# Tail of a graph-attention and mixture-of-experts kernel: the last down projection in other banks by halves, its hidden rows turned inside expert 6's projection, two gathered blocks scaled by ScalarE

## What is computed

```python
xf = _layernorm(x.reshape(-1, Dd), ln_g, ln_b)
scores, idx = jax.lax.top_k(xf @ router_w, K)          # K = 2
gate = jax.nn.softmax(scores, axis=-1)
...
def _expert(x, g, b, W1, b1, W2, b2, Wo, bo):
    x = _layernorm(x, g, b)
    x1 = x @ W1 + b1
    x2 = jnp.clip(x @ W2 + b2, -20.0, 20.0)
    hidden = jnp.clip(x1 * (x2 * jax.nn.sigmoid(x2)), -10000.0, 10000.0)
    return jnp.clip(hidden @ Wo + bo, -10000.0, 10000.0)
...
out = sum over experts of gates_e[:, e, None] * _expert(xf, ...)
x = x + out
```

## Time and profile before

| | us |
|---|---|
| median of 3 executions | 535.42 |
| lowest, highest | 532.96, 538.06 |
| profiled execution, its own time | 531.92 |
| its span, first to last instruction | 530.0 |
| TensorE busy in the span | 502.4 |
| VectorE busy | 397.4 |
| ScalarE busy | 285.5 |
| GpSimd busy | 187.2 |

### The profile page before, as it was taken

One profiled execution on the slowest core, in us unless ns is written; L12 is line 12 of the kernel. 1 busy time (PEld: TensorE's weight loads), 2 busy tenths in 40 slices (PEclk: granted clock), 3 DMA queues, 4 the chain that ended last, 5 costly groups with the idle time before them and its releaser, 6 DMA issues.

```text
span 530.0 us, 6969 instructions
## 1 busy us (share of the span) xinstructions
PE 502.4 (95%) x2647; PEld 445.7 (84%) x2647; DVE 397.4 (75%) x652; ACT 285.5 (54%) x408; POOL 187.2 (35%) x168
## 2 busy tenths in 40 slices
PE   8999999999999999999999999769999999999985
PEld 8999999999999978788888887647887877877774
DVE  4848989953535335589887876886898898998996
ACT  4724134241342416498886216436788688697641
POOL 5000535665566003279885822150020000000363
PEclk9999999999999999999999999759999999999989
DMA  8489754444243442202006452475969989889463
GB/s 306 145 322 344 217 195 156 156 159 160 84 155 126 158 160 72 88 1 81 0 1 239 165 208 91 150 240 221 351 231 403 349 353 406 335 321 398 145 215 121
DMA packets 21075, 106.34 MB, mean 201 GB/s; under 512 B 4865, under 2 KB 5249, under 8 KB 11313
## 3 DMA queue, kind: packets, MB, share of 16 engines
q1 hardware_dynamic: 15472, 91.53, 46.1%
q0 software_dynamic: 3696, 7.96, 4.6%
q10 hardware_dynamic: 1872, 6.39, 3.6%
HBM read 98.97 MB, written 6.91 MB: 200 GB/s over the span
## 4 chain that ended last, share of the span: by engine, by line
PE 60%; DVE 21%; ACT 11%; DMA 3%; issue 3%; POOL 1%; SPq 0%; ACTq 0%; POOLq 0%; DVEq 0%
PE ps L1165 51%; DVE lo L757 12%; ACT hi L575 4%; ACT xg L674 3%; PE ps L1232 3%; PE ps L1171 2%; DMA raw<-in_wg 2%; PE ps L1260 2%; DVE eqt L844 1%; ACT xg_hi L678 1%; DMA xg<-z_rows,slot_tok 1%; DVE x2sg L1078 1%; DMA z_rows<-xfb 1%; PE ps L1297 1%; ACT x2sg L683 1%
## 5 line engine op out<-in xcount | busy, mean ns | idle before, releaser
L757 DVE TENSOR_TENSOR lo<-raw,hi 128x2048 fp32r<-128x2048 f32 x70 | 161.3, 2326 | 42.6 <-ACT hi L575 42.3
L575 ACT ACTIVATE hi<-raw 128x2048 fp32r<-128x2048 f32 x70 | 131.6, 1913 | 59.4 <-PE ps L1165 49.1
L460 POOL DMA_INDIRECT mask_rows<-colf,bits x48 | 61.9, 1290 | 92.3 <-DVE bits L852 44.1
L487 POOL TENSOR_SCALAR pr<-pr,small 128x384 f32<-128x384 f32 x48 | 59.0, 1247 | 54.6 <-DVE small L866 54.6
L1165 PE MATMUL ps<-xt_hi,lo 128*128 128x384 f32 x176 | 59.1, 336 | 0.0
L1165 PE MATMUL ps<-xt_hi,hi 128*128 128x384 f32 x176 | 59.1, 336 | 0.0
L1165 PE MATMUL ps<-xt_lo,hi 128*128 128x384 f32 x176 | 59.1, 336 | 0.0
L1165 PE MATMUL ps<-hi,xg_hi 128*128 128x512 f32 x128 | 52.0, 406 | 5.7 <-DVE lo L757 3.9
L1165 PE MATMUL ps<-lo,xg_hi 128*128 128x512 f32 x128 | 51.3, 401 | 0.0
L1165 PE MATMUL ps<-hi,xg_lo 128*128 128x512 f32 x128 | 51.3, 401 | 0.0
L1165 PE MATMUL ps<-t_hi,hi 128*128 128x384 f32 x128 | 43.1, 337 | 0.9 <-DVE t_lo L803 0.9
(11 more groups left out here) (221 smaller groups left out, 1078.2 us busy)
## 6 DMA issues: line engine op xcount, KB each, us to landing
raw<-in_wf SPq DMA_DIRECT2D x42, 1024.0 KB, 6.9
raw<-in_wg SPq DMA_DIRECT2D x28, 1024.0 KB, 4.9
xfb<-in_wf SPq DMA_DIRECT2D x6, 1024.0 KB, 7.4
src_i<-in_srcb ACTq DMA_DIRECT2D x4, 768.0 KB, 3.9
dst_i<-in_dstb ACTq DMA_DIRECT2D x4, 768.0 KB, 7.6
y_rows<-y SPq DMA_DIRECT2D x6, 512.0 KB, 3.0
xin<-in_x SPq DMA_DIRECT2D x3, 512.0 KB, 4.3
xres<-in_x SPq DMA_DIRECT2D x3, 512.0 KB, 4.2
```

The lines of the kernel that those rows point to most:

```text
L460: pool.indirect_dma_start(out=mbuf[:, :], out_offset=bass.IndirectOffsetOnAxis(ap=bits[:, 1, g:g + 1], axis=0), in_=colf[:, 5, g:g + 1], i ...
L487: pool.tensor_scalar(pr[:, h % 3, i, :], pr[:, h % 3, i, :], rinv[:, h % 3, i:i + 1], None, ALU.mult).then_inc(normalised, 1)
L575: act.activation(hi[SLOT[c]][:, :], raws[RAW[c]], ACT.Copy).then_inc(hi_done, 1)
L757: dve.tensor_tensor(lo[SLOT[c]][:, :], raws[RAW[c]], f32(hi[SLOT[c]][:, :]), ALU.subtract).then_inc(lo_done, 1)
```

## The change

Six things are changed, all in the tail. `down(7)` writes to B[1] and B[0] in place of B[3] and B[4], and no longer waits for `y_ready`; the sums of tile 0 go to B[3] and B[4] in place of B[0] and B[1]. `turn_hidden(7)` moves from behind `down(6)` to between its two halves. VectorE's `split_lo(75)` moves from in front of `hidden_lo(7)`, `store_y(6)` and the gate copy to behind them. Expert 7's clip is done by halves, each as soon as its half of the projection is done, with `y_rest` of the first half between them. Gathered blocks 0 and 1, rather than 4 and 5, are scaled by ScalarE and added by GpSimd; VectorE adds 2 to 5, and their places in its list change. ScalarE does its two scalings before, rather than after, the copies of `last_slots` and `y_hi` of expert 6. GpSimd's two additions stay behind all six gathers.

```diff
-        SUM_BANKS = [(0, 1), (5, 6), (2, 7)]
+        SUM_BANKS = [(3, 4), (5, 6), (2, 7)]
+        LAST_Y = [B[1], B[0]]
...
-                    for n in (4, 5):
+                    for n in (0, 1):
                         t, j = GATHERS[n]
-                        pool.wait_ge(rows_scaled, n - 3)
+                        pool.wait_ge(rows_scaled, n + 1)
                         ins = pool.tensor_tensor(xres[:, t, :], xres[:, t, :], yg[:, YG_SLOT[n], :], ALU.add)
...
             turned_hi(NE - 1, (NE - 1) % 2)
 
+            act.wait_ge(most_ready, 1)
+            for n in (0, 1):
+                t, j = GATHERS[n]
+                act.wait_ge(y_rows_in[j][t], 16)
+                act.activation(yg[:, YG_SLOT[n], :], yg[:, YG_SLOT[n], :], ACT.Copy, scale=r3[:, 8 + j, t:t + 1]).then_inc(rows_scaled, 1)
             act.wait_ge(last_oh_turned, 1)
...
-            act.wait_ge(most_ready, 1)
-            for n in (4, 5):
-                t, j = GATHERS[n]
-                act.wait_ge(y_rows_in[j][t], 16)
-                act.activation(yg[:, YG_SLOT[n], :], yg[:, YG_SLOT[n], :], ACT.Copy, scale=r3[:, 8 + j, t:t + 1]).then_inc(rows_scaled, 1)
...
                 dve.tensor_scalar(hh[:, :], hh[:, :], 10000.0, -10000.0, ALU.min, ALU.max).then_inc(h_ready, 1)
+                if e == NE - 1:
+                    split_lo(CHUNKS - 2)
+                    hidden_lo(NE - 1, (NE - 1) % 2)
+                    store_y(NE - 2, (NE - 2) % 2)
+                    dve.wait_ge(last_oh_turned, 1)
+                    dve.tensor_copy(slot_gate, B[7][:, 0:2]).then_inc(slot_gates, 1)
+                    split_lo(CHUNKS - 1)
+                    break
...
+            def last_y(half):
+                dve.wait_ge(chunk_used, CHUNKS - 1 + half)
+                dve.tensor_scalar(y[:, 1, halves[half]], LAST_Y[half], 10000.0, -10000.0, ALU.min, ALU.max).then_inc(y_half, 1)
+
+            def last_add(half, t):
+                dve.wait_ge(last_summed, NT * half + t + 1)
+                if t == 0:
+                    dve.wait_ge(tile_added, 1)
+                dve.tensor_tensor(xres[:, t, halves[half]], xres[:, t, halves[half]], B[SUM_BANKS[t][half]],
+                                  ALU.add).then_inc(out_ready, 1)
+
+            last_y(0)
             dve.wait_ge(y_hi_done, 1)
             y_rest(0, slice(0, D))
...
+            dve.wait_ge(y_hi_done, 2)
+            y_rest(1, halves[0])
+            last_y(1)
+            add_rows(2)
+            dve.wait_ge(y_hi_done, 3)
+            y_rest(1, halves[1])
+            for n in range(3, 6):
+                add_rows(n)
             for half in range(2):
                 for t in range(NT):
...
+                    last_add(half, t)
...
             def down(e, par, c):
+                to = LAST_Y if e == NE - 1 else B[3:5]
                 pe.wait_ge(ht_lo_done, e + 1)
-                if e:
+                if e and e < NE - 1:
                     pe.wait_ge(y_ready, e)
...
                     ins.then_inc(chunk_used, 1)
+                    if e == NE - 2 and part == 0:
+                        turn_hidden(NE - 1)
...
-                turn_hidden(e)
...
+                if e < NE - 1:
+                    turn_hidden(e)
+            turn_slots()
             down(NE - 1, 1, CHUNKS - 2)
```

More of the change, by code:

```diff
@@ L544, in _ @@
                         gather_rows(n)
-                    for n in (4, 5):
+                    for n in (0, 1):
                         t, j = GATHERS[n]
-                        pool.wait_ge(rows_scaled, n - 3)
+                        pool.wait_ge(rows_scaled, n + 1)
                         ins = pool.tensor_tensor(xres[:, t, :], xres[:, t, :], yg[:, YG_SLOT[n], :], ALU.add)
-                        if n == 4:
+                        if n == 0:
                             link(ins)
@@ L1104, in y_rest @@
                                          op0=ALU.mult, op1=ALU.subtract).then_inc(y_lo_done, 1)
[L1106 to L1111, removed]
+            halves = [slice(0, CW), slice(CW, D)]
+            def last_y(half):
[8 more added lines that the diff above has]
+            last_y(0)
             dve.wait_ge(y_hi_done, 1)
             y_rest(0, slice(0, D))
[L1114 to L1121, removed]
+            dve.wait_ge(y_hi_done, 2)
[6 more added lines that the diff above has]
+                add_rows(n)
             for half in range(2):
                 for t in range(NT):
[L1124 to L1128, removed]
+                    last_add(half, t)
             dve.wait_ge(out_ready, 2 * NT)
@@ L1361, in down @@
                     cols = slice(D + part * CW, D + (part + 1) * CW)
-                    pe.matmul(B[3 + part], selx[:, e % 3, :], brow[:, cols], start=True, stop=False)
+                    pe.matmul(to[part], selx[:, e % 3, :], brow[:, cols], start=True, stop=False)
                 for part in range(2):
@@ L1365, in down @@
                     for k in range(HT):
-                        ins = three(B[3 + part], (ht_hi[:, par, k, :], ht_lo[:, par, k, :]), weight(c + part, k), False, k == HT - 1)
+                        ins = three(to[part], (ht_hi[:, par, k, :], ht_lo[:, par, k, :]), weight(c + part, k), False, k == HT - 1)
                     ins.then_inc(chunk_used, 1)
+                    if e == NE - 2 and part == 0:
+                        turn_hidden(NE - 1)
             def turn_hidden(e):
@@ L1375, in turn_hidden, with turn_slots @@
                 ins.then_inc(h_turned, 1)
+            def turn_slots():
+                pe.wait_ge(last_oh, 1)
+                pe.wait_ge(xg_scaled, 2 * NE)
+                for j in range(2):
+                    for t in range(NT):
+                        pe.transpose(B[5 + j][:, t * P:(t + 1) * P], last_rows[:, j, t, :], ident[:, :])
+                for j in range(2):
+                    for t in range(NT):
+                        ins = pe.matmul(B[7][:, j:j + 1], last_rows[:, j, t, :], gates[:, t, LAST[j]:LAST[j] + 1], start=t == 0, stop=t == NT - 1)
+                ins.then_inc(last_oh_turned, 1)
             turn_tokens(0, 0)
```

## The result

Over 18 executions of each kernel the median goes from 533.41 to 536.63 us; the ratio is 1.0058, 95% interval 1.0037 to 1.0079, which is 3.1 us (2.0 to 4.2) of 533.41. The profiled execution takes 536.84 us (span 535.1) against 531.92.

What follows compares the result with a forecast made beforehand. VectorE, not TensorE, was taken as the bound: with no turn lost to GpSimd -0.6 us, with the turns worked out +2.7 us. Added to the 535.42 us median this gave 538.1 us, range 533.3 to 541.5.

Steps and rivals of the forecast that it cites:

- the rival without a collision: In the tail, GpSimd's additions and VectorE do not exclude each other: -0.6 us, 534.8 us, chance 0.13.
- the rival of a low clock: TensorE is granted 1.2 GHz from the new pause at 503.57 to the end: +5.5 us, 540.9 us, chance 0.07.
- Hidden, as said: ScalarE's earlier scalings and later copies add no time, unless block 1 lands later than 508.7.
- The sixth gather: On GpSimd, it starts at 510.26, 0.26 us after split_lo(75), and ends 0.8 us behind it, at 513.05.
- The rival with the gather in front: GpSimd's sixth gather precedes split_lo(75) and ends at 511.2; GpSimd's first addition ends at 514.5: +1.7 us, 537.1 us, chance 0.14.
- The collision: GpSimd's two additions take turns with VectorE's y_rest instructions, which wait for them: +2.7 us, 538.1 us, chance 0.66.
- VectorE's standing still in front of the first clip: VectorE waits for down(6) and the gate products, 1.3 us in all, with no add_rows to fill it.
- TensorE's sums: TensorE's sums before the final additions are done by 523 in any of the cases.
- The end: VectorE's six final additions end at 529.5, against 526.8 before.

Runs made afterwards that it cites:

- the run without the late add_rows: The changed kernel without GpSimd's two additions and without VectorE's add_rows of blocks 3, 4 and 5: tail 19.07 us, 528.71 us in one run.
- the run with TensorE's part alone: The kernel before with the change's new `down`, `turn_hidden`, `turn_slots` and their banks, other lists as before: tail 22.16 us, ratio to before 0.9979.
- the run with five blocks on VectorE: The changed kernel with VectorE adding five gathered blocks in another order and GpSimd only block 5, late: tail 21.15 us, ratio to before 0.9974.

## Why the prediction was right

The time, 536.63 us, lies in the range, and the change was forecast at +2.7 us: the tail shows +2.70. The range is wide enough for the rival without a collision too (534.8), so it is the steps below that tell the mechanism. The absolute 538.1 was 1.5 us too high, because the median of three executions that I added to, 535.42, lies 2.0 above that of 18, 533.41; the ratio of the times gives +3.1.

Step by step, with 2.34 us taken off the times after:

- TensorE: the transposes begin at 504.53 (504.62 expected), down(7) at 509.70 (509.86), its first half is clipped from 513.26 (513.2), its last product ends at 516.02 (516.0). The clock stayed at 1.00 in it, so the rival of a low clock did not occur.
- ScalarE: the second scaling ends at 508.79 (508.9 to 509.3), y_hi of expert 6 at 511.79 (511.9). Hidden, as said.
- The sixth gather starts at 510.28, 0.33 us behind split_lo(75), and takes 2.77 us in place of 0.94, ending 0.82 us behind the split. The rival with the gather in front did not occur in any of the five traces in which the two stand this way. The inference of the Trainium skill that the prediction weighed (SBUF — State Buffer, Who interferes with whom), that a tensor_tensor leaves descriptor making alone, does not hold for these gathers: 2.77 against 0.94 us. Whether the making of descriptors is held or the reading of the row numbers, which lie in SBUF, no run tells.
- The collision: turns at 515.48, 516.58, 518.84 and 519.39 (515.5, 516.6, 518.85, 519.4). Without it the tail is 22.23, 0.54 shorter than before (0.6 expected).
- VectorE's standing still in front of the first clip: 0.71, 0.67 and 1.02 us, 2.40 in all. The prediction's 1.3 us leave out the third wait; its sum goes by the times, which have it.
- TensorE's sums end at 523.69, later than the 523 that the prediction gave for every case, but 2 us ahead of the final additions.
- The end: 529.51 (529.5).

So two things make the result. VectorE comes last: the run without the late add_rows shows that its list bounds the tail, and the run with TensorE's part alone that the projection, which ends 2.6 us earlier (11.98 us behind the hh instruction with the change, 14.55 before), shortens the tail by only 0.61 us. And the two engines hold each other up: without GpSimd's additions the tail of the changed kernel is 3.24 us shorter.

This does not mean that the collision alone is the loss, since before had a hold too. What follows is an estimate from the timelines. Call idle the time in their brackets, and held what an instruction takes over the same shape unheld. VectorE is idle for 2.04 us of the tail before and for 2.40 after; it is held for 1.39 and for 3.58. What is left, its own work, is 19.3 and 19.5 us, and between 19.3 and 19.6 in every other run in which it has the same work. So longer holds make 2.2 of the 2.70 us. With TensorE's part alone, in the old order, VectorE is idle for only 0.20 us and held for about 2.7: against that the changed lists add 2.2 us of idle time and 0.9 us of holds. So the new order, which puts no add_rows in front of the first clip, has a price of its own. The run with five blocks on VectorE fits this: it fills that stretch, avoids the holds, and has the shortest tail of all the runs that do the whole work.

Not tried: the kernel before, or TensorE's part alone, without GpSimd's additions, which would show how the loss divides between order and collision; and VectorE's new order with GpSimd's additions neither left out nor moved but made by another engine.

## What to carry to other kernels

Before speeding up the engine that stands last on a chain, count what the next engine has still to do behind that point: work that was hidden under the slow step moves onto the path, instruction by instruction. Where VectorE and GpSimd both work on SBUF, lay their lists side by side and put GpSimd's two-input work beside VectorE's PSUM work or waits; an instruction whose duration varies twofold at the same shape, ending a fixed time behind one of the other engine, is the sign that they hold each other. Where such work is moved to the very end, check that the engine's closing does not then end the program later. When only the tail is changed, measure from a common mark in the trace, as what comes in front can move by more than the change.

## What the traces show of the hardware

Issuing a gather, which moves its data by DMA, is held by a VectorE instruction with two SBUF tensors: 0.94 us alone, 2.77 us when begun 0.33 us behind a 2.28 us split, ending about 0.8 us behind the instruction that held it in all these traces. The reverse was not seen: three add_rows take 3.92 us beside a gather and 3.92 with none beside them.

An instruction that gets its turn after waiting is shorter than its full duration counted from the release: 0.55 in place of 0.75 us for 128x512 on VectorE, 1.10 in place of 1.28 us for 128x1024, 2.26 in place of 2.41 us on GpSimd.

GpSimd's closing DRAIN ends 5.2 us behind its last addition: at 527.0 with the addition's end at 521.76 before, at 530.7 with 525.48 with five blocks on VectorE. The prediction had the first two of these from the rows, not the third.
